# Cross attention: a longer ring of key chunks, both copies of the keys' high part in one load, and a head's output four pairs later

## The chip, the cores and the metric

The kernel runs on one core of a Trainium2 chip. The time is the device time of one execution in microseconds (us), from the first to the last instruction with what lies around it. The engines are named as in the profile: PE is TensorE (PEld its weight loads), DVE is VectorE, ACT is ScalarE, POOL is GpSimd, and SP is SyncE, which here only issues DMAs.

## The reference

The program is a perceiver of two layers on 512 latent rows of 512 numbers. Each layer has a cross attention to a context of 8192 rows, a mixer (a selective scan in layer 0, linear attention in layer 1), and a feed-forward part with experts. The change touches the two cross attentions alone. With 16 heads of 32 numbers they compute

```python
# layer 0, and layer 1 without the mask
energy = jnp.einsum('nqhd,nkhd->nhqk', q, k)
energy = jnp.where(mask == 0, jnp.float32(-1e+20), energy)
attention = jax.nn.softmax(energy / scale, axis=3)
out = jnp.einsum('nhql,nlhd->nqhd', attention, v).reshape(n, q_len, EMBED)
return out @ Wo.T + bo
```

All of it is in float32. Keys and queries are split into a high and a low part. The product is taken as one matmul over 98 rows (QROWS + 2): three groups of 32 rows hold the keys as high, high, low and the queries as high, low, high. The two last rows take away the largest score of each query.

## The kernel before

A head's 8192 keys are cut into 16 chunks of 512 (NKC), and a chunk into two pairs of 128-key tiles, so a head has 32 pairs (PAIRS, `p` from 0 to 31). For each chunk PE does four matmuls for the row maxima (`maxima`, line 588), which run 17 chunks (NKC + LEAD) ahead of its four matmuls for the scores (`scores`, line 610, in layer 0 each behind one that adds the mask, line 609). DVE reduces the maxima (line 744 in layer 1, 748 in layer 0). ACT takes the exponentials of a pair into one of `n_p` buffers called `prob` (line 698). PE multiplies them with the values once per chunk (`wave`, line 623).

The sums of the exponentials (the denominators) are taken over pairs. POOL adds most pairs itself (lines 855 and 858). The others it hands to DMAs that add into `den_dma` (lines 847 and 851): 9 of 32 pairs in layer 0, and 13 in layer 1 with two accumulators. At the start of the next head, one DMA for each accumulator adds it into `den_pool` (`merge`, line 836). A `prob` buffer is free again when its wave and its addition are done.

The keys lie in HBM as a high and a low matrix. SP loads each chunk into a slot of `k_ring` (`load_k`, line 544): three loads of 32 rows of 2 KB, two of them the same high rows. The ring has 19 slots (KRING), and chunk n + 19 is loaded when the scores of chunk n are done. PE needs it at the start of chunk n + 2. At chunk 1 of each head SP also loads the queries of the head after next (line 535) and the next head's values (line 550, 1 MB). All of SP's loads go through one queue. POOL's additions by DMA go through another, and both are served by the same 16 DMA engines.

When a head's waves are over, `head_out` (line 636, at pair 8 of the next head) turns its output and sums the denominators. It waits for the merges. ACT copies the result (`head_rows`, line 709), and DVE adds the parts at pair 11 (`den_sum`), with a division every fourth head (line 777).

Each engine's order is the order of its own function in the code. Engines wait for each other by semaphores alone.

Of the kernel before, what the change touches and what calls it, by code (L numbers as in the profile page):

```python
# [30 lines left out]
LEAD = 1  # L31
KRING = NKC + LEAD + 2
KT = S2 // P
# [444 lines left out]
def cross_attention(k, ctx, q_hi_lo, k_hi_lo, v_heads, v_first, w_out, bias, x_rows, comb, scale, masks, attT):  # L478
# [7 lines left out]
    rows_m = slice(QROWS, QROWS + 2)  # L486
    n_q, n_p = 3, 6 if masked else 8
    q_stack = [k.sbuf(ctx, "q_stack", [QROWS + 2, T], F32R) for _ in range(n_q)]
    k_ring = k.sbuf(ctx, "k_ring", [QROWS + 2, KRING, KC], F32R)
    v_buf = [v_first[:].rearrange("p k n -> p (k n)"), k.x[:].rearrange("p i d -> p (i d)")]  # L490
# [5 lines left out]
    den_dma = [k.sbuf(ctx, "den_dma", [P, 2, T], F32) for _ in range(sums.n_acc)]  # L496
    small = k.sbuf(ctx, "bias_and_m_hi", [QROWS + 2, T], F32)
    bias_row, m_hi = small[0:1, :], small[rows_m, :].bitcast(F32R)
    den4 = k.sbuf(ctx, "den_of_4_heads", [P, T], F32)
    lo_sign = k.sbuf(ctx, "lo_sign", [QROWS + 2, 1], F32)  # L500
    o_sb = k.sbuf(ctx, "o_sb", [P, T], F32)

    s_k = [k.sem("s_k") for _ in range(KRING)]
    s_v = [k.sem("s_v") for _ in range(2)]
# [22 lines left out]
    with nc.Block() as block:  # L527
        @block.sync
        def _(e):
# [8 lines left out]
            def load_k(n):  # L538
                h, c = divmod(n, NKC)
                rows = slice(h * DH, (h + 1) * DH)  # L540
                if n >= KRING:
                    e.wait_ge(s_score, 2 * (n - KRING) + 2)
                for g, part in enumerate((0, 0, 1)):
                    e.dma_start(k_ring[g * DH:(g + 1) * DH, n % KRING, :].bitcast(F32),
                                k_hi_lo[part][rows, chunk_cols(c)]).then_inc(s_k[n % KRING], 16)

# [5 lines left out]
            load_q(0)  # L552
            for n in range(KRING):
                load_k(n)
            load_q(1)
            load_v(0)
            for n in range(NCH):
                h, c = divmod(n, NKC)
                if n + KRING < NCH:
                    load_k(n + KRING)  # L560
                if c == 1 and h + 2 < H:
                    load_q(h + 2)
                if c == 1 and h == H - 1:
                    e.wait_ge(s_wave, WAVES * (H - 1))
                    e.dma_start(v_first[:], w_out).then_inc(s_wo, 16)
                    e.dma_start(bias_row, bias).then_inc(s_bo, 16)
                elif c == 1:
                    load_v(h + 1)
            e.wait_ge(s_wave, WAVES * H)
            e.dma_start(k.x[:], x_rows).then_inc(s_xback, 16)  # L570
# [3 lines left out]
        def _(e):  # L574
            def maxima(n, i):
                h, c = divmod(n, NKC)
                if i == 0:
                    if c == 0:
                        e.wait_ge(s_q[h % n_q], 48 * (h // n_q + 1))
                    if c == 0 and h >= n_q:  # L580
                        e.wait_ge(s_zero, h - n_q + 1)
                    if n < KRING:
                        e.wait_ge(s_ring, n_q + n + 1)
                    e.wait_ge(s_k[n % KRING], 48 * (n // KRING + 1))
                if 4 * n + i >= 2:
                    e.wait_ge(s_red, 4 * n + i - 1)

                e.matmul(k.bank(maxbank[i % 2]), q_stack[h % n_q][:, i * P:(i + 1) * P], k_ring[:, n % KRING, :],  # L588
                         start=True, stop=True).then_inc(s_max, 1)
# [9 lines left out]
            def scores(g):  # L599
# [6 lines left out]
                for j in range(2):  # L606
                    kt = 2 * j2 + j
                    if masked:
                        e.matmul(k.bank(kt), k.ident_big[:], masks[1][:, 2 * p + j, :], start=True, stop=False)  # L609
                    ins = e.matmul(k.bank(kt), k_ring[:, n % KRING, kt * P:(kt + 1) * P], q_stack[h % n_q][:],  # L610
                                   start=not masked, stop=True)
# [32 lines left out]
            for g in range(H * PAIRS):  # L644
# [12 lines left out]
                if p == PAIRS - 2 and h + 1 < H:  # L657
                    max_rows(h + 1)
                if p == 8 and h > 0:
                    head_out(h - 1)  # L660
# [16 lines left out]
        def _(e):  # L677
            mask_rows = k.i["mask"].rearrange("(i p) k -> p i k", p=P)

            def m_hi_rows(h):  # L680
                e.wait_ge(s_topT, h + 1)
                if h > 0:
                    e.wait_ge(s_mlo, h)
                e.activation(m_hi, misc[rows_m, :], ACT.Copy).then_inc(s_mhi, 1)

# [36 lines left out]
            for g in range(H * PAIRS):  # L722
# [4 lines left out]
                if p == 1 and h > 0:  # L727
                    take_values(h - 1)
                if p == 8 and h > 0:
                    head_rows(h - 1)  # L730
# [4 lines left out]
        def _(e):  # L735
# [23 lines left out]
            def m_lo_rows(h):  # L759
                e.wait_ge(s_mhi, h + 1)  # L760
                if h >= n_q:
                    e.wait_ge(s_score, reused_stack(h))
                e.scalar_tensor_tensor(out=q_stack[h % n_q][rows_m, :], in0=small[rows_m, :], scalar=lo_sign[rows_m, :],
                                       in1=misc[rows_m, :], op0=ALU.mult, op1=ALU.add).then_inc(s_mlo, 1)
# [29 lines left out]
            for g in range(H * PAIRS):  # L794
# [11 lines left out]
                if p == 3 and n_q <= h + 2 < H:  # L806
                    zero_rows(h + 2)
                if p == 11 and h > 0:
                    den_sum(h - 1)
# [10 lines left out]
        def _(e):  # L820
# [3 lines left out]
            for b in range(n_q):  # L824
                e.memset(q_stack[b][rows_m, :].bitcast(F32), 0.0).then_inc(s_ring, 1)
            for n in range(KRING):
                e.memset(k_ring[rows_m, n, :].bitcast(F32), -1.0).then_inc(s_ring, 1)
            e.wait_ge(s_ring, n_q + KRING)

# [1878 lines left out]
```

## Time and profile before

| | us |
|---|---|
| median of 3 runs | 4746.3 (4741.35 to 4748.71) |
| the profiled execution, its own time | 4741.35 |
| its span, first to last instruction | 4739.6 |
| layer 0, cross attention, first matmul of line 588 to last of line 610 | 406.0 to 1591 |
| layer 1, the same | 2691.9 to 3802.6 |

The profile is of the fastest of the three runs, and 1.75 us of its time lie around the span. The span's busy shares are PE 87%, PEld 47%, DVE 64%, ACT 45%, POOL 44%. The granted TensorE clock is 0.92 of full speed over the span. A row of a timeline reads: start, duration, engine, line, operation, tiles written and read, and in brackets how long the engine had been idle and for what.

### The profile page before, as it was taken

Reading aid. Unit: us, or ns where it says so; the run is one execution under the profiler, and the core shown is the slowest. Engines: PE = TensorE matmul, PEld = TensorE weight load, DVE = VectorE, ACT = ScalarE, POOL = GpSimd, SP = SyncE. Lnnn points to the kernel's source line nnn. Section 1 sums busy time; section 2 is a strip of 40 time slices with the busy share of each in tenths; the row PEclk is TensorE's granted clock in tenths of the full one; section 3 lists DMA queues with packets and bytes.
Section 4 is the critical chain, followed back from the end, with each engine's and each line's share of the span. In section 5 each row is a group of like instructions: output and inputs, shape, how many; then the busy total and the mean of one; then the engine's idle time right before and its main releaser. Section 6 shows DMA issues by size and latency. Waiting matters only on the chain. (4 is left out here: it accounts for less than half of the span.)

```text
span 4739.6 us, 50995 instructions
## 1 busy us (share of the span) xinstructions
PE 4103.6 (87%) x17384; PEld 2236.5 (47%) x17384; DVE 3035.5 (64%) x5059; ACT 2130.9 (45%) x2348; POOL 2068.5 (44%) x1208
## 2 busy tenths in 40 slices
PE   8995999999999686689999588888888879669997
PEld 6883444443434251157777343333333323347775
DVE  4335777777777259945777476666766543377776
ACT  2220444554545333324767145455555623146675
POOL 0000788888889616400000168778887920000000
PEclk9996999999999779889999789899998979889998
DMA  8997565665655300024888468778887840307876
GB/s 299 338 330 257 125 141 128 142 144 128 142 136 131 102 13 0 0 82 154 303 302 311 146 144 186 174 176 186 175 190 179 179 111 0 99 9 281 304 301 234
DMA packets 294006, 803.62 MB, mean 170 GB/s; under 512 B 47475, under 2 KB 81011, under 8 KB 256372
## 3 DMA queue, kind: packets, MB, share of 16 engines
q1 hardware_dynamic: 223764, 561.77, 34.7%
q0 software_dynamic: 61280, 221.80, 23.3%
q10 hardware_dynamic: 8704, 16.78, 1.1%
q8 instruction: 141, 2.31, 0.2%
q14 instruction: 117, 0.96, 0.1%
HBM read 485.81 MB, written 98.37 MB: 123 GB/s over the span
## 5 line engine op out<-in xcount | busy, mean ns | idle before, releaser
L588 PE MATMUL psum<-k_ring,q_stack 98*128 98x512 f32 x2048 | 916.5, 471 | 218.6 <-DMA k_ring<-k_lo 132.9
L858 POOL TENSOR_TENSOR den_pool<-den_pool,prob 128x1024 f32<-128x1024 f32 x418 | 1022.2, 2445 | 146.4 <-ACT prob L698 128.0
L698 ACT ACTIVATE prob<-psum 128x1024 f32<-128x1024 f32 x726 | 741.9, 1024 | 697.1 <-PE psum L610 658.5
L744 DVE TENSOR_REDUCE row_max<-psum 128x1 f32<-128x512 f32 x1024 | 682.5, 689 | 326.8 <-PE psum L588 322.6
L748 DVE CUSTOM_DVE_ANT_0 psum<-psum,mask_q 128x512 f32<-128x512 f32 x1024 | 703.1, 707 | 291.4 <-PE psum L588 289.7
L610 PE MATMUL psum<-q_stack,k_ring 98*128 98x512 f32 x2048 | 884.3, 504 | 2.8 <-ACT prob L698 2.5
L588 PEld LDWEIGHTS psum<-k_ring,q_stack 98*128 98x128 f32 x2048 | 409.2, 200 | 932.7 <-issue 339.0
L1814 DVE TENSOR_TENSOR weight_lo<-weight_raw,weight_hi 128x2048 fp32r<-128x2048 f32 x240 | 547.0, 2290 | 162.2 <-ACT weight_hi L1757 161.9
L858 POOL TENSOR_TENSOR den_pool<-den_pool,xnT 128x1024 f32<-128x1024 f32 x190 | 465.0, 2447 | 62.2 <-ACT xnT L698 52.3
L1757 ACT ACTIVATE weight_hi<-weight_raw 128x2048 fp32r<-128x2048 f32 x240 | 453.9, 1915 | 39.3 <-DMA weight_raw<-in_L_ffn_w 22.4
L698 ACT ACTIVATE xnT<-psum 128x1024 f32<-128x1024 f32 x298 | 304.7, 1024 | 297.6 <-PE psum L610 276.8
L610 PEld LDWEIGHTS psum<-q_stack,k_ring 98*128 98x128 f32 x2048 | 413.0, 203 | 47.2 <-ACT prob L698 17.6
L609 PE MATMUL psum<-mask_k,ident_big 128*128 128x512 fp8e4 x1024 | 405.9, 396 | 6.9 <-ACT xnT L698 5.0
L1670 POOL DMA_DIRECT2D y_slots<-xnT x30 | 16.4, 545 | 878.9 <-ACT xnT L1779 878.9
L1256 PE MATMUL psum<-dB_u,ident 128*128 128x512 f32 x256 | 156.3, 710 | 99.5 <-DVE dB_u L1231 99.3
L1217 POOL TENSOR_TENSOR dB_u<-delta_u,B_all 128x2048 f32<-128x2048 f32 x32 | 144.2, 4513 | 196.9 <-POOLq L1099 109.5
L847 POOL DMA_DIRECT2D den_dma<-prob x228 | 204.0, 895 | 52.3 <-ACT prob L698 31.2
L609 PEld LDWEIGHTS psum<-mask_k,ident_big 128*128 128x128 bf16 x1024 | 100.9, 99 | 245.4 <-issue 213.9
L104 PE MATMUL psum<-weight_hi,hidden_T_hi 128*128 128x512 f32 x480 | 199.1, 415 | 3.8 <-DVE weight_lo L1814 3.5
L104 PE MATMUL psum<-weight_hi,slot_x_hi 128*128 128x512 f32 x480 | 201.6, 420 | 0.0
L623 PE MATMUL psum<-prob,v_then_wo 128*32 128x512 f32 x1448 | 201.3, 629 | 0.0
L623 PE MATMUL psum<-prob,x 128*32 128x512 f32 x1456 | 196.9, 613 | 0.0
(398 smaller groups left out, 6354.1 us busy)
## 6 DMA issues: line engine op xcount, KB each, us to landing
den_dma<-prob POOLq DMA_DIRECT2D x254, 512.0 KB, 5.0
weight_raw<-in_L_ffn_w SPq DMA_DIRECT2D x120, 1024.0 KB, 6.5
k_ring<-k_hi SPq DMA_DIRECT2D x1024, 64.0 KB, 2.7
weight_raw<-in_L_ffn_Wu SPq DMA_DIRECT2D x60, 1024.0 KB, 7.1
weight_raw<-in_L_ffn_Wd SPq DMA_DIRECT2D x60, 1024.0 KB, 5.0
den_dma<-xnT POOLq DMA_DIRECT2D x98, 512.0 KB, 4.9
k_ring<-k_lo SPq DMA_DIRECT2D x512, 64.0 KB, 2.6
den_pool<-den_dma POOLq DMA_DIRECT2D x48, 512.0 KB, 5.6
```

The lines of the kernel that those rows point to most:

```text
L104: ins = e.matmul(out, lhsT, rhs, start=start and n == 0, stop=stop and n == len(terms) - 1)
L588: e.matmul(k.bank(maxbank[i % 2]), q_stack[h % n_q][:, i * P:(i + 1) * P], k_ring[:, n % KRING, :], start=True, stop=True).then_inc(s_max, 1)
L609: e.matmul(k.bank(kt), k.ident_big[:], masks[1][:, 2 * p + j, :], start=True, stop=False)
L610: ins = e.matmul(k.bank(kt), k_ring[:, n % KRING, kt * P:(kt + 1) * P], q_stack[h % n_q][:], start=not masked, stop=True)
L623: ins = e.matmul(vbank[n * DH:(n + 1) * DH, :], v_buf[h % 2][:, t * DH:(t + 1) * DH], prob[(PAIRS * h + t // 2) % n_p][:, t % 2, :], start ...
L698: e.activation(prob[g % n_p], k.psum[:, 2 * j2:2 * j2 + 2, :], ACT.Exp, scale=scale).then_inc(s_exp, 1)
L744: e.reduce_max(out, bank, AXIS_X).then_inc(s_red, 1)
L748: e.tensor_tensor_reduce(out=bank, in0=bank, in1=masks[0][:, i, chunk_cols(c)], scale=1.0, scalar=-3.0e38, op0=ALU.add, op1=ALU.max, accum ...
L847: e.dma_start(den_dma[a][:], tile, accum_op=ALU.add).then_inc(s_ddma[a], 16)
L858: e.tensor_tensor(den[:], den[:], tile, ALU.add).then_inc(s_dpool, 1)
L1757: e.activation(hi[q % RING][:], raw[q % RAW][:], ACT.Copy).then_inc(s_whi, 1)
L1814: e.tensor_tensor(lo[q % RING][:], raw[q % RAW][:], hi[q % RING][:].bitcast(F32), ALU.subtract).then_inc(s_wlo, 1)
```

## The change

- The ring gets 20 slots in layer 0 and 32 in layer 1. In layer 1 `n_p` goes from 8 to 10.
- The two loads of the same high rows become one, whose source names the 32 rows twice (`to_broadcast([2, DH, KC])`, a first dimension of size 2 and step 0). Its destination is the first 64 rows of the slot. The slot's semaphore then counts two loads.
- `head_out` and `head_rows` move from pair 8 to pair 12, `den_sum` and the division from pair 11 to 15.
- The tile `small` is gone. ACT writes the rounded maximum straight into the rows of `q_stack`, where DVE reads it and puts the remainder in its place. Two waits go with it. The bias row is loaded into a part of `den_pool` at the end of the last head.
- POOL sets the two last rows of each slot once at the start: 20 and 32 memsets in place of 19 each.

```diff
--- before.py
+++ after.py
-KRING = NKC + LEAD + 2
...
-    n_q, n_p = 3, 6 if masked else 8
+    n_q, n_p = 3, 6 if masked else 10
+    kring = NKC + LEAD + (3 if masked else 15)
     q_stack = [k.sbuf(ctx, "q_stack", [QROWS + 2, T], F32R) for _ in range(n_q)]
-    k_ring = k.sbuf(ctx, "k_ring", [QROWS + 2, KRING, KC], F32R)
+    k_ring = k.sbuf(ctx, "k_ring", [QROWS + 2, kring, KC], F32R)
...
-    small = k.sbuf(ctx, "bias_and_m_hi", [QROWS + 2, T], F32)
-    bias_row, m_hi = small[0:1, :], small[rows_m, :].bitcast(F32R)
+    bias_row = den_pool[0][0:1, 0, :]
...
-                if n >= KRING:
-                    e.wait_ge(s_score, 2 * (n - KRING) + 2)
-                for g, part in enumerate((0, 0, 1)):
-                    e.dma_start(k_ring[g * DH:(g + 1) * DH, n % KRING, :].bitcast(F32),
-                                k_hi_lo[part][rows, chunk_cols(c)]).then_inc(s_k[n % KRING], 16)
+                if n >= kring:
+                    e.wait_ge(s_score, 2 * (n - kring) + 2)
+                hi, lo = (part[rows, chunk_cols(c)] for part in k_hi_lo)
+                e.dma_start(k_ring[0:2 * DH, n % kring, :].bitcast(F32), hi.unsqueeze(0).to_broadcast([2, DH, KC])
+                            ).then_inc(s_k[n % kring], 16)
+                e.dma_start(k_ring[2 * DH:QROWS, n % kring, :].bitcast(F32), lo).then_inc(s_k[n % kring], 16)
...
                     e.dma_start(v_first[:], w_out).then_inc(s_wo, 16)
-                    e.dma_start(bias_row, bias).then_inc(s_bo, 16)
                 elif c == 1:
                     load_v(h + 1)
+            e.wait_ge(s_head, H - 1)
+            e.dma_start(bias_row, bias).then_inc(s_bo, 16)
...
-                    e.wait_ge(s_k[n % KRING], 48 * (n // KRING + 1))
+                    e.wait_ge(s_k[n % kring], 32 * (n // kring + 1))
...
-                if p == 8 and h > 0:
+                if p == 12 and h > 0:
                     head_out(h - 1)
...
-                if h > 0:
-                    e.wait_ge(s_mlo, h)
-                e.activation(m_hi, misc[rows_m, :], ACT.Copy).then_inc(s_mhi, 1)
+                e.activation(q_stack[h % n_q][rows_m, :], misc[rows_m, :], ACT.Copy).then_inc(s_mhi, 1)
...
-                if p == 8 and h > 0:
+                if p == 12 and h > 0:
                     head_rows(h - 1)
...
-                if h >= n_q:
-                    e.wait_ge(s_score, reused_stack(h))
-                e.scalar_tensor_tensor(out=q_stack[h % n_q][rows_m, :], in0=small[rows_m, :], scalar=lo_sign[rows_m, :],
+                m_rows = q_stack[h % n_q][rows_m, :]
+                e.scalar_tensor_tensor(out=m_rows, in0=m_rows.bitcast(F32), scalar=lo_sign[rows_m, :],
                                        in1=misc[rows_m, :], op0=ALU.mult, op1=ALU.add).then_inc(s_mlo, 1)
...
-                if p == 11 and h > 0:
+                if p == 15 and h > 0:
                     den_sum(h - 1)
...
-            for n in range(KRING):
+            for n in range(kring):
                 e.memset(k_ring[rows_m, n, :].bitcast(F32), -1.0).then_inc(s_ring, 1)
```

SP's queue at the start of layer 0's cross attention, before. A row is an operation with its destination, source and the destination's shape:

```order
L535 DMA q_stack<-q_hi 32x512
L535 DMA q_stack<-q_lo 32x512
L535 DMA q_stack<-q_hi 32x512
L544 DMA k_ring<-k_hi 32x512 x2
L544 DMA k_ring<-k_lo 32x512
L544 DMA k_ring<-k_hi 32x512 x2
L544 DMA k_ring<-k_lo 32x512
L544 DMA k_ring<-k_hi 32x512 x2
```

and now:

```order
L534 DMA q_stack<-q_hi 32x512
L534 DMA q_stack<-q_lo 32x512
L534 DMA q_stack<-q_hi 32x512
L543 DMA k_ring<-k_hi 64x1x512
L545 DMA k_ring<-k_lo 32x512
L543 DMA k_ring<-k_hi 64x1x512
L545 DMA k_ring<-k_lo 32x512
L543 DMA k_ring<-k_hi 64x1x512
```

The two loads of 32 high rows have become one to 64 rows, and line numbers are one less.

ACT in head 1 of layer 0 before, from the exponentials of pairs 2 and 3 (in `xnT`, two of the `prob` buffers) to head 0's output rows (`attT` and `den_of_heads`):

```order
L698 ACTIVATE xnT<-psum 128x1024 x2
L698 ACTIVATE prob<-psum 128x1024 x4
L698 ACTIVATE xnT<-psum 128x1024
L709 ACTIVATE attT<-psum 32x512
L712 ACTIVATE den_of_heads<-psum 32x512
L698 ACTIVATE xnT<-psum 128x1024
```

and now:

```order
L697 ACTIVATE xnT<-psum 128x1024 x2
L697 ACTIVATE prob<-psum 128x1024 x4
L697 ACTIVATE xnT<-psum 128x1024 x2
L697 ACTIVATE prob<-psum 128x1024 x3
L708 ACTIVATE attT<-psum 32x512
L711 ACTIVATE den_of_heads<-psum 32x512
L697 ACTIVATE prob<-psum 128x1024
```

Four more exponentials stand ahead of the head's output rows. PE's `head_out` moves in the same way.

## Rows read from the trace of the kernel before

**Rows 1.** The profile's page: the span and the costliest group.
```profile
span 4739.6 us, 50995 instructions
...
L588 PE MATMUL psum<-k_ring,q_stack 98*128 98x512 f32 x2048 | 916.5, 471 | 218.6 <-DMA k_ring<-k_lo 132.9
```

**Rows 2.** Busy time by stretch: 14 heads of layer 0, 14 of layer 1.
```profile
core 0: us, PE busy (x) PEld busy (x) DVE busy (x) ACT busy (x) POOL busy (x), PEclk, DMA share, GB/s
552.70:1537.00 984.30, 940.43 (x4674) 404.17 (x4673) 710.35 (x1859) 491.80 (x504) 844.81 (x448) 0.99 0.60 137
2809.80:3755.50 945.70, 831.19 (x3777) 366.21 (x3775) 651.27 (x968) 491.85 (x504) 765.98 (x462) 0.93 0.80 181
```

**Rows 3.** PE's waits, 500 to 1550 us (total, times, longest).
```profile
PE psum L588 <- DMA k_ring<-k_lo: 28.7, 26, 3.0
```

**Rows 4.** PE's waits, 2790 to 3790 us.
```profile
PE psum L588 <- DMA k_ring<-k_lo: 71.4, 50, 4.9
PE psum L636 <- DMA den_pool<-den_dma: 18.8, 13, 6.2
```

**Rows 5.** Timeline of SP, layer 1: start, duration; a chunk is released between them.
```profile
3115.57 1.51 SPq L544 DMA_DIRECT2D k_ring<-k_hi  x2
...
3118.97 1.44 SPq L544 DMA_DIRECT2D k_ring<-k_hi  x2
```

**Rows 6.** Timeline of SP, layer 0, the same.
```profile
597.75 0.77 SPq L544 DMA_DIRECT2D k_ring<-k_hi  x2
...
601.75 0.77 SPq L544 DMA_DIRECT2D k_ring<-k_hi  x2
```

**Rows 7.** Timeline, layer 1, chunks 1 to 4 of a head.
```profile
3022.15 0.53 SPq L550 DMA_DIRECT2D x<-v_heads  x1
...
3023.78 0.50 PE L588 MATMUL psum<-k_ring,q_stack 98*128 98x512 f32 x1 [0.96 <-DMA k_ring<-k_lo]
...
3029.21 0.50 PE L588 MATMUL psum<-k_ring,q_stack 98*128 98x512 f32 x1 [1.96 <-DMA k_ring<-k_lo]
...
3031.95 1.03 PE L636 MATMUL psum<-o_sb,comb 128*32 128x512 f32 x1 [1.54 <-DMA den_pool<-den_dma]
```

**Rows 8.** DMA queues (packets, MB, share of 16), layer 0, 500 to 1550 us.
```profile
q0 software_dynamic: 21600, 78.65, 38.4%
q1 hardware_dynamic: 38326, 64.96, 21.6%
```

**Rows 9.** DMA queues, layer 1 (2790 to 3790 us).
```profile
q0 software_dynamic: 32167, 117.16, 59.5%
q1 hardware_dynamic: 37106, 62.96, 20.4%
```

**Rows 10.** DMA, 2700 to 2720 us: packets by size, loads issued.
```profile
DMA packets 1881, 2.73 MB, mean 137 GB/s; under 512 B 624, under 2 KB 624, under 8 KB 1857
...
k_ring<-k_hi SPq DMA_DIRECT2D x22, 64.0 KB, 2.1
...
k_ring<-k_lo SPq DMA_DIRECT2D x12, 64.0 KB, 2.0
```

**Rows 11.** DMA, 2121.9 to 2126.5 us: packets by size.
```profile
DMA packets 321, 0.18 MB, mean 39 GB/s; under 512 B 48, under 2 KB 304, under 8 KB 320
```

**Rows 12.** DMA, 2204.4 to 2207 us: packets, and a load of two rows.
```profile
DMA packets 37, 0.27 MB, mean 106 GB/s; under 512 B 2, under 2 KB 2, under 8 KB 4
...
up_b_row<-up_bias SPq DMA_DIRECT2D x1, 4.0 KB
```

**Rows 13.** DMA queue of SP, 2300 to 2600 us (weights).
```profile
q1 hardware_dynamic: 12430, 89.17, 79.7%
```

**Rows 14.** DMA queue of SP, 100 to 300 us (context).
```profile
q1 hardware_dynamic: 46821, 65.54, 94.5%
```

**Rows 15.** Timeline of POOL, layer 1, last head: first and last additions.
```profile
3758.50 2.39 POOL L855 TENSOR_TENSOR den_pool<-prob 128x1024 f32<-128x1024 f32 x1
...
3809.77 5.56 POOL L858 TENSOR_TENSOR den_pool<-den_pool,xnT 128x1024 f32<-128x1024 f32 x2
```

## What the change should do to the time

> **What bounds the kernel now.** I read three views: busy time by stretch, then what PE waited for in each stretch, then the DMA queues. The chain that ended last covers only the final normalization and says nothing here. The page names line 588 as PE's costliest group, with 132.9 of its 218.6 us of idle time spent waiting for keys [rows 1]. The first view gives the time of a head. From the first score of head 1 to that of head 15, layer 0 takes 984.3 us and layer 1 945.7 us for 14 heads each: POOL's 448 instructions are 14 times 32 and its 462 are 14 times 33. That is 70.3 and 67.6 us a head [rows 2]. PE is busy 96% of layer 0's stretch and 88% of layer 1's, and the granted clock is 0.99 and 0.93.
>
> An undisturbed chunk shows in SP's own timeline. The load of a chunk goes out when the scores of one are done, so two of these starts lie a chunk apart: 3.40 us in layer 1 [rows 5] and 4.00 us in layer 0 [rows 6]. Sixteen make 54.4 and 64.0 us, so 13 us a head in layer 1 and 6 us in layer 0 are something else. The second view says what. PE stood idle for keys 28.7 us in 26 places of layer 0 [rows 3], and 71.4 us in 50 places of layer 1, where it also waited 18.8 us for the merges [rows 4]. The timeline shows one such place. SP issues the 1 MB of values, the keys behind them come late twice (0.96 and 1.96 us), and at pair 8 the head's output waits 1.54 us for a merge [rows 7]. So a longer ring and a later output aim at waits that are there.
>
> The third view decides the case. In layer 1 POOL's queue takes 59.5% of the 16 DMA engines and SP's queue 20.4% [rows 9]; in layer 0 it is 38.4% and 21.6% [rows 8]. The engines have room as long as each load spreads over all of them.
>
> **The double load.** How many engines a load used can be read from the packets. Between 2700 and 2720 us SP issued 38 loads (34 of keys, 3 of queries, 1 of values), and 624 packets were under 512 B, though no data of these loads is that small [rows 10]. That is 16 a load: each engine that takes part ends with one small packet. At 2122 us stand two loads of 128 rows and two of 8 rows, and the small packets are 48, which is 2 times 16 and 2 times 8 [rows 11]. A load of two rows leaves two small packets and two of data [rows 12]. So the engines follow the first dimension: 8 rows use 8 engines, 2 rows use 2. The new load has 64 rows at its destination, but its source's first dimension is 2. No load of before has two sides that differ so. I take the smaller, two engines, since the small first dimensions in these rows set the number each time.
>
> The Trainium skill, "DMA: Bandwidth & Descriptors", in "Why a DMA increments its semaphore by 16 and not by 1", says that a DMA runs on the largest number up to 16 that divides the first dimension (size 1 left out) of both sides, and its "Rules for kernel authors" name this very case: a leading broadcast of c copies confines the whole DMA to at most c engines. It would give two engines, and rows 10 to 12 agree with it where both sides are alike.
>
> The cost is the work of those two engines. Each moves half of the 128 KB of a chunk, 0.0655 MB, and 1.049 MB a head. One engine's time for 1 MB follows from a queue's share times 16 times the stretch, over its MB. With weights it is 0.797 x 16 x 300 / 89.17 = 42.9 us [rows 13], with the context 0.945 x 16 x 200 / 65.54 = 46.1 us [rows 14], and in layer 1 now 0.204 x 16 x 1000 / 62.96 = 51.8 us [rows 9]. A head's double loads then take 45.0, 48.4 or 54.4 us of each of the two engines. I take 45.0, the price under a queue that never runs dry, because this one won't.
>
> The rest of their work stays. POOL's queue takes 0.595 x 67.6 = 40.2 us a head in layer 1 and 0.384 x 70.3 = 27.0 us in layer 0. SP's queue takes 13.8 and 15.2 us, of which the high keys are 2.10 of 4.39 MB (48 loads of 64 KB, 3 of queries, 1 MB of values), so 7.2 and 7.9 us are left. The sums are 40.2 + 7.2 + 45.0 = 92.4 us a head in layer 1, and 27.0 + 7.9 + 45.0 = 79.9 us in layer 0. Both are above the 67.6 and 70.3 us of now. A ring can bridge a late load but not a rate, so the two engines set the pace: a chunk every 5.8 and 5.0 us. Keys of 240 of the 256 chunks are due in the 15 heads after the start, hence 15 x 24.8 = 372 us in layer 1 and 15 x 9.6 = 144 us in layer 0.
>
> **The other parts.** The longer ring and the two added `prob` buffers would take away the waits for keys, but not under this rate: nothing. The later output lies four pairs behind the merge's landing; its 18.8 us are also inside heads that the two engines now stretch: nothing. SP issues two loads for three; its queue is not late. Dropping `small` leaves ACT's and DVE's instructions as many and as wide as before. The 13 more memsets of layer 1 run while PE goes through the 17 first chunks, 58 us. The bias row goes out at pair 12 of the last head, over 30 us before its matmul. All of these count nothing, and if one does cost, it is under 5 us. The division every fourth head (three waits of DVE's maxima in each layer) moves with its pair and stays.
>
> The sum against the profiled execution (4741.35 us, its span 4739.6) is 4741 + 372 + 144 = 5257 us; I say 5260. The median of the runs is 5 us above that execution, which is well inside the range.
>
> **Rivals.** *All 16 engines serve the double load* (12 in 100). The destination's 64 rows would decide it. Nothing in rows 10 to 12 excludes this for two unlike sides. Then the waits go. POOL alone needs 3758.50 to 3815.3 = 56.8 us for layer 1's last head, where it hardly waits [rows 15], and PE needs 54.4 us and some 3 for the change of heads, the output and the division. With 2 us of leftovers a head takes 59.5 us, 8.1 less. Layer 0 comes to 64.0 + 4 = 68.0, 2.3 less. That is 15 x 10.4 = 156 us: 4585 us, faster.
>
> *Two engines, but not the bound* (6 in 100). If an engine served SP's packets while one of POOL's adding packets waits, its time would be the larger of the two and not the sum: 7.2 + 45.0 = 52 us a head, under 59.5. Against it stands that no queue's share plus the other's passes 100% in any row I have. The time would be some 4600 to 4650 us, faster. It decides from the point where the sum falls below 67.6 us, that is where under 20 of POOL's 40.2 us exclude SP's.
>
> *Two engines, and the clock goes too* (inside the forecast's case, its upper end). PE would wait 1 to 2 us in each chunk. Now the clock is already 0.93 in layer 1, where waits are more frequent, against 0.99 [rows 2]. In layer 1 a slower PE hides behind 5.8 us a chunk. In layer 0, 5.0 us leave 1.0 us over the 4.00, and a part of the chunks would run longer.
>
> **How the numbers follow.** The forecast's case, that two engines set the pace, has 80 in 100. Its own bounds are these. With the dearest price, 54.4, the heads take 101.8 and 89.3 us, which gives 4741 + 513 + 285 = 5540. With 45.0 and a tenth of the work overlapping on an engine, they take 83.2 and 71.9 us, or 4741 + 234 + 24 = 5000. The range is 5000 to 5550, and it leaves out the two faster rivals. The last 2 in 100 go to offsets that cancel. A measurement of this kernel tells about 0.2% from no change, 10 us. So faster has 0.18, same 0.01, slower 0.81.
>
> **What would show it.** If I am right, small packets of SP's queue fall to 2 + 16 a chunk instead of 48. The double load lands after 5 us and more where one took 2.1 [rows 10]. Line 588 waits for `k_ring` in nearly every chunk, longer in layer 1. Starts of SP's key loads lie 5 to 6 us apart, POOL waits for ACT, and the DMA share falls although two engines are full. If line 588 hardly waits, and heads take about 60 us in layer 1, the first rival is right and my step on the source's first dimension is wrong. If small packets show 2 engines and heads still take 60 to 67 us, it is the second: adding packets and loads overlap.

## The result and the profile after

The changed kernel takes 5128.1 us (median of 4 runs, 5120.59 to 5139.64), the kernel before beside it 4747.51 us (4741.35 to 4751.46). The ratio is 1.0805, with a 95% interval of 1.0779 to 1.0831. The profiled execution took 5120.59 us, 379 more than that of before. The forecast was 5260 us with a range of 5000 to 5550.

The page of the changed kernel: span, packets, and PE's costliest group ([rows 1] before). Line 588 of before is 589 here, 610 is 611, 636 is 637, 698 is 697, and SP's key loads stand in lines 543 and 545.

```profile
span 5118.5 us, 50455 instructions
...
DMA packets 278641, 803.50 MB, mean 157 GB/s; under 512 B 32115, under 2 KB 65652, under 8 KB 241013
...
L589 PE MATMUL psum<-k_ring,q_stack 98*128 98x512 f32 x2048 | 947.2, 489 | 403.2 <-DMA k_ring<-k_lo 227.1
```

Packets under 512 B were 47475 before and are 32115 now. The difference is 15360, which is 512 chunks times 30, so a chunk leaves 18 small packets for 48. That is 16 for the low keys and 2 for the double load: two engines carry it, as the third view of the kernel before had suggested. PE's idle time ahead of the maxima rose from 218.6 to 403.2 us.

Busy time by stretch, from the first score of head 1 to that of head 15 in each layer ([rows 2] before):

```profile
core 0: us, PE busy (x) PEld busy (x) DVE busy (x) ACT busy (x) POOL busy (x), PEclk, DMA share, GB/s
582.70:1665.60 1082.90, 982.49 (x4674) 415.96 (x4673) 709.99 (x1859) 485.09 (x504) 848.66 (x447) 0.95 0.52 125
2980.00:4129.70 1149.70, 897.11 (x3776) 400.41 (x3774) 647.68 (x968) 490.66 (x504) 782.30 (x467) 0.83 0.62 149
```

A head takes 1082.9 / 14 = 77.4 us in layer 0 (70.3 before) and 1149.7 / 14 = 82.1 us in layer 1 (67.6 before). The DMA share fell, from 0.60 and 0.80 to 0.52 and 0.62, although the kernel waits more. An average over 16 engines hides two that are full. The trace's own packets, taken from start to end, show this. In the changed kernel's stretch of layer 1 fewer than two packets are under way at once in under 0.1% of the time, and exactly two in 32%. In the kernel before it was 14% and 1%. The granted clock is 0.95 and 0.83, for 0.99 and 0.93.

DMA of layer 1, heads 1 to 13: packets, MB and share of 16 engines; then KB and median us to landing ([rows 9] before).

```profile
q0 software_dynamic: 28469, 103.64, 46.6%
q1 hardware_dynamic: 26898, 56.14, 15.5%
...
den_dma<-prob POOLq DMA_DIRECT2D x136, 512.0 KB, 7.8
...
v_then_wo<-v_heads SPq DMA_DIRECT2D x7, 1024.0 KB, 16.4
```

These 1079.4 us hold 13 heads of 83.0 us. POOL's queue takes 0.466 x 83.0 = 38.7 us of each engine, SP's 0.155 x 16 x 83.0 = 206 us of all together. Taking away the 7.2 us an engine that I had put down for SP's other loads (115 us on 16) leaves 91 us for the double load, or 45.4 us on each of its two engines. The forecast had used 45.0. The sum is 38.7 + 7.2 + 45.4 = 91.3 us, and the head takes 83.0: about a tenth of the work overlaps. This is an estimate, because no view separates the double loads from SP's other loads.

What PE and SP waited for in that layer (total, times, longest; [rows 4] before):

```profile
PE psum L589 <- DMA k_ring<-k_lo: 122.1, 54, 4.4
PE psum L589 <- DMA q_stack<-q_hi: 80.5, 12, 10.2
PE psum L637 <- DMA den_pool<-den_dma: 20.6, 14, 9.2
```

```profile
SPq L543 <- PE psum L611: 33.5, 57, 2.2
```

SP waits for a free chunk of the ring in only 33.5 of 1150 us. Something else holds it, and its timeline (start, duration) shows what:

```profile
3686.59 7.53 SPq L545 DMA_DIRECT2D k_ring<-k_lo  x1
3694.16 0.51 SPq L543 DMA_DIRECT2D k_ring<-k_hi  x1
3694.71 4.46 SPq L545 DMA_DIRECT2D k_ring<-k_lo  x1
3699.51 0.51 SPq L543 DMA_DIRECT2D k_ring<-k_hi  x1
...
3705.91 5.92 SPq L545 DMA_DIRECT2D k_ring<-k_lo  x1
...
3712.43 6.39 SPq L545 DMA_DIRECT2D k_ring<-k_lo  x1
```

An issue of low keys that takes 0.43 us when the queue is short takes up to 7.53 us here; over the whole run the median is 1.86 us and the longest 8.98 us, where the longest issue of a key load was 2.24 us in the kernel before. SP is held while it issues. I read this as the double loads ahead of it not having gone yet. Everything that SP issues later stands behind them. That is why PE also waited 80.5 us in 12 places for the queries of a coming head (`q_stack`), a wait that the kernel before did not have in layer 1, and why the 1 MB of values lands after 16.4 us.

In layer 0 the picture is another one. There SP does wait for the ring, and ACT waits for the sums:

```profile
SPq L543 <- PE psum L611: 782.5, 218, 9.5
```

```profile
ACT prob L697 <- DMA den_dma<-prob: 155.2, 44, 5.9
...
ACT xnT L697 <- DMA den_dma<-xnT: 60.1, 19, 5.7
```

ACT cannot reuse a buffer of `prob` before POOL's adding transfer has read it. Such a transfer lands after 6.9 us in layer 0 where it took 4.8 before (median). I read this as its slices on the two engines standing behind the double loads. ACT waits 215 us for them; in the kernel before, over the same 14 heads, all waits of ACT for these transfers came to 20 us. The two engines are nearly as full in this layer: fewer than two packets are under way in 1.8% of its stretch, and in 30% before.

### The profile page after: what moved, and what is told of

The parts are those of the page before. It is cut to its first block and busy times, and to the rows that moved or that the text cites. A ratio compares the mean times of both kernels' runs of the same rounds, so it can differ in the third digit from the quotient of the medians.

```text
span 5118.5 us, 50455 instructions
## 1 busy us (share of the span) xinstructions
PE 4224.2 (83%) x17384; PEld 2286.7 (45%) x17384; DVE 3033.0 (59%) x5059; ACT 2122.9 (41%) x2348; POOL 2091.6 (41%) x1222
## 2 busy tenths in 40 slices
DMA packets 278641, 803.50 MB, mean 157 GB/s; under 512 B 32115, under 2 KB 65652, under 8 KB 241013
## 5 line engine op out<-in xcount | busy, mean ns | idle before, releaser
L589 PE MATMUL psum<-k_ring,q_stack 98*128 98x512 f32 x2048 | 947.2, 489 | 403.2 <-DMA k_ring<-k_lo 227.1
L856 POOL TENSOR_TENSOR den_pool<-den_pool,prob 128x1024 f32<-128x1024 f32 x444 | 1133.8, 2554 | 173.6 <-ACT prob L697 154.1
L697 ACT ACTIVATE prob<-psum 128x1024 f32<-128x1024 f32 x752 | 765.0, 1024 | 1014.2 <-PE psum L611 817.8
L611 PE MATMUL psum<-q_stack,k_ring 98*128 98x512 f32 x2048 | 929.0, 527 | 4.8 <-ACT prob L697 3.7
L589 PEld LDWEIGHTS psum<-k_ring,q_stack 98*128 98x128 f32 x2048 | 426.3, 209 | 1132.9 <-issue 433.9
L611 PEld LDWEIGHTS psum<-q_stack,k_ring 98*128 98x128 f32 x2048 | 435.9, 214 | 53.9 <-ACT prob L697 19.5
L856 POOL TENSOR_TENSOR den_pool<-den_pool,xnT 128x1024 f32<-128x1024 f32 x164 | 416.0, 2537 | 43.1 <-ACT xnT L697 34.1
L697 ACT ACTIVATE xnT<-psum 128x1024 f32<-128x1024 f32 x272 | 277.2, 1024 | 329.4 <-PE psum L611 237.6
L1668 POOL DMA_DIRECT2D y_slots<-xnT x30 | 16.4, 545 | 878.1 <-ACT xnT L1777 878.1
L624 PE MATMUL psum<-prob,x 128*32 128x512 f32 x1512 | 220.4, 658 | 1.4 <-ACT prob L697 1.4
L624 PE MATMUL psum<-prob,v_then_wo 128*32 128x512 f32 x1496 | 219.8, 662 | 0.0
```

Source lines behind the costliest of these rows:

```text
L611: ins = e.matmul(k.bank(kt), k_ring[:, n % kring, kt * P:(kt + 1) * P], q_stack[h % n_q][:], start=not masked, stop=True)
L624: ins = e.matmul(vbank[n * DH:(n + 1) * DH, :], v_buf[h % 2][:, t * DH:(t + 1) * DH], prob[(PAIRS * h + t // 2) % n_p][:, t % 2, :], start ...
L697: e.activation(prob[g % n_p], k.psum[:, 2 * j2:2 * j2 + 2, :], ACT.Exp, scale=scale).then_inc(s_exp, 1)
L856: e.tensor_tensor(den[:], den[:], tile, ALU.add).then_inc(s_dpool, 1)
```

## Experiments

The theory to test (A): the double load's first dimension of 2 puts it on two DMA engines, and these set the pace. The rivals: the ring or the later output costs the time (B); the row that is read twice, or a load of 64 rows, is slow in itself (C). Medians are of 4 runs or more, each compared with the kernel before on the same chip (4741 to 4750 us). "A head" is again the stretch from the first score of head 1 to that of head 15, divided by 14, layer 0 then layer 1.

| kernel | us | ratio (95%) | a head |
|---|---|---|---|
| changed kernel | 5128 | 1.0805 (1.0779-1.0831) | 77.4, 82.1 |
| three loads | 4616 | 0.9730 (0.9708-0.9751) | 67.9, 60.6 |
| double load alone | 5485 | 1.1572 (1.1531-1.1613) | 90.5, 94.4 |
| copies side by side | 4611 | 0.9719 (0.9700-0.9738) | 67.8, 59.8 |
| first dimension 2 | 5163 | 1.0885 (1.0859-1.0912) | 77.2, 84.7 |
| first dimension 4 | 4744 | 0.9989 (0.9975-1.0003) | 69.3, 67.6 |
| first dimension 8 | 4637 | 0.9781 (0.9758-0.9804) | 67.9, 60.6 |
| ring alone, three loads | 4675 | 0.9842 (0.9818-0.9866) | 67.9, 65.0 |
| later output alone, three loads | 4719 | 0.9939 (0.9917-0.9961) | 71.0, 65.2 |
| changed, ring 19 in both | 5498 | 1.1580 (1.1552-1.1609) | 92.4, 92.7 |
| changed, rings 22 and 23 | 5139 | 1.0824 (1.0797-1.0851) | 78.2, 83.4 |
| changed, early output | 5131 | 1.0814 (1.0785-1.0842) | 78.0, 81.8 |
| changed, values early | 5127 | 1.0806 (1.0780-1.0831) | 78.5, 83.0 |

### Three loads again

```diff
-    e.dma_start(k_ring[0:2 * DH, n % kring, :]..., hi.unsqueeze(0).to_broadcast([2, DH, KC]))
+    for g in range(2):
+        e.dma_start(k_ring[g * DH:(g + 1) * DH, n % kring, :]..., hi)
```

> The changed kernel with its double load split again into two loads of 32 rows; the rings of 20 and 32 chunks, the two more buffers of prob and the output at pair 12 stay. Theory A (two DMA engines carry the double load and set the pace): all of the loss goes with this one edit. The small packets are 48 a chunk again (about 47500 in all), a head takes 70 us or less in layer 0 and 60 to 67 us in layer 1, and the time is 4600 to 4760 us. Rival B (the longer ring, whose 32 chunks go out ahead of the queries and the values, or the later output costs the time): it stays at 5050 us or more.

4615.81 us, 512 us under the changed kernel. Its page, and its windows:

```profile
DMA packets 294006, 803.61 MB, mean 174 GB/s; under 512 B 47475, under 2 KB 81012, under 8 KB 256373
```

```profile
core 0: us, PE busy (x) PEld busy (x) DVE busy (x) ACT busy (x) POOL busy (x), PEclk, DMA share, GB/s
554.40:1504.50 950.10, 934.98 (x4674) 402.55 (x4673) 711.70 (x1859) 491.79 (x504) 846.84 (x448) 0.99 0.62 142
2779.40:3627.60 848.20, 789.65 (x3777) 352.94 (x3775) 661.16 (x968) 491.81 (x504) 770.26 (x461) 0.97 0.87 199
```

The small packets are the 47475 of before, the DMA share in layer 1 is 0.87, and the ring with the later output is worth 128 us over the kernel before. B is out: all of the loss goes with this one line.

### The double load alone

The kernel before with the changed kernel's two loads for its three (ring 19, 8 buffers of `prob` in layer 1, output at pair 8).

```diff
-    for g, part in enumerate((0, 0, 1)):
-        e.dma_start(k_ring[g * DH:(g + 1) * DH, n % KRING, :]..., k_hi_lo[part][rows, chunk_cols(c)])
+    e.dma_start(k_ring[0:2 * DH, n % KRING, :]..., hi.unsqueeze(0).to_broadcast([2, DH, KC]))
+    e.dma_start(k_ring[2 * DH:QROWS, n % KRING, :]..., lo)
```

> The kernel before with the double load alone: ring of 19 chunks, 8 buffers of prob in layer 1, output at pair 8. Theory A: the small packets are 18 a chunk, a head takes about 77 us in layer 0 and 83 us in layer 1, as in the changed kernel, and the time is 5080 to 5200 us: the start of layer 1, where the changed kernel loses 31 us behind its 32 chunks, should cost less, and the shorter ring should cost some of it back. Rival B (ring or output): 4740 to 4780 us.

5485.18 us, above the range that I gave. The double load costs 741 us by itself, and the other parts of the change give 357 us of that back. The forecast had counted them as nothing under the double load. The experiment on the ring, below, takes this up.

### The copies side by side

```diff
-    hi.unsqueeze(0).to_broadcast([2, DH, KC])      # source dimensions 2, 32, 512
+    hi.unsqueeze(1).to_broadcast([DH, 2, KC])      # source dimensions 32, 2, 512
```

The queries' high and low rows go to even and odd rows of `q_stack` to match.

> The changed kernel, with the two copies of a row written beside each other: the one load still reads each high row twice and moves the same bytes, but its source's first dimension is 32 and the copies are the second one. The queries' high and low rows are laid out in the same order. Theory A: 16 engines take part, the small packets are 32 a chunk (about 39300 in all), and the time is that of three loads or a little less, 4600 to 4760 us. Rival C (reading one row twice, or one load of 64 rows, is what is slow): it stays at 5050 us or more.

```profile
DMA packets 285808, 803.53 MB, mean 174 GB/s; under 512 B 39283, under 2 KB 72819, under 8 KB 248180
```

4610.54 us. It is still one load that reads each row twice and writes 64 rows, and the bytes are the same. The small packets are 39283, which is 7168 = 512 x 14 more than in the changed kernel: 32 a chunk for 18, so 16 for this load. C is out as well. This is the fastest kernel of the study, 2.8% under the kernel before, though level with three loads within the intervals: a load fewer a chunk is worth nothing that can be told here.

### First dimension 2, 4 and 8, no row read twice

Two plain loads of the high keys, whose source is only taken in another order of rows (a = 2, 4, 8; `q_stack` laid out alike):

```diff
+    for g in range(2):
+        e.dma_start(k_ring[g * DH:(g + 1) * DH, n % kring, :]..., hi.rearrange("(b a) n -> a b n", a=2))
```

> The changed kernel with two plain loads of the high keys and no row read twice by one load, but each load's rows are taken in an order that makes its source's first dimension 2 (even rows, then odd rows; the queries' first two groups are laid out alike). Theory A, with both loads on the same two engines: 20 small packets a chunk (about 33100 in all) and a time like the changed kernel's, 5050 to 5200 us. If loads of two engines fall on different engines each time, the packets are the same and the time is 4600 to 4800 us. Rival C (a row read twice is what is slow): 4600 to 4760 us with 48 small packets a chunk.

5162.91 us: as slow as the changed kernel and 35 us more, without any repeated row. The added time lies in layer 1 (84.7 us a head for 82.1), and no view tells what of it is the extra load and what the queries. The small packets:

```profile
DMA packets 278772, 803.53 MB, mean 156 GB/s; under 512 B 32243, under 2 KB 65779, under 8 KB 241140
```

They are 32243, 128 more than the changed kernel's: the extra load adds 2 a chunk (+1024), and the 64 loads of queries that were taken in the same order leave 2 each for 16 (-896). I had left the queries out of the expectation's 33100. That separate loads do not fall on separate pairs is concluded from the time: 84.7 us a head in layer 1, where four engines for each load give 67.6 in the next run.

> As the two plain loads whose first dimension was 2, with 4. Theory A: four engines carry each load, the small packets are 24 a chunk (about 33500 in all, with the queries' 64 loads at 4 for 16), and the work on each of the four is half: 40.2 + 7.2 + 22.5 = 69.9 us a head in layer 1 if nothing overlaps, about 61 with the overlap that the pair showed (83.2 for 92.4), so that they hardly bound. The time is 4630 to 4760 us. Rival (the order of the rows, and not the number of engines, is slow): 5000 us or more.

4744.28 us. The packets, and what PE waited for in layer 1:

```profile
DMA packets 280949, 803.56 MB, mean 169 GB/s; under 512 B 34419, under 2 KB 67955, under 8 KB 243316
```

```profile
PE psum L641 <- DMA den_pool<-den_dma: 84.9, 11, 9.9
```

34419 small packets are 2304 above the changed kernel's: 6 a chunk (3072) less 12 for each of 64 loads of queries (768). So four engines carry each load. The packets under way say so too: exactly four in 16% of layer 1's stretch, and in 2% of the changed kernel's. Four do not bound the keys any more, but they still make the sums late: PE waits 84.9 us for merges, against 17.7 us with three loads. A head takes 67.6 us where I had estimated about 61. The time is inside the range, at its upper end.

> As the two plain loads whose first dimension was 2 and 4, with 8. Eight engines carry each load; with four it was 4744 us and with 16 it was 4616 us. Theory A: what an engine has to do is halved again, and the time is 4625 to 4680 us; the small packets are 32 a chunk, about 38800 in all. Rival (any order of rows but the plain one costs the same 128 us): 4730 to 4750 us.

4636.61 us, with 38771 small packets. Compared through the kernel before, eight engines cost 0.5% over sixteen (0.9781 to 0.9730). The loss falls with the number of engines: with 2, 4 and 8 it is 547, 128 and 21 us over three plain loads by the medians, and 548, 123 and 24 us compared through the kernel before.

### Ring alone and later output alone, with three loads

The first is the changed kernel with three loads and the output back at pair 8. It keeps the rings of 20 and 32 chunks, the 10 buffers of `prob` in layer 1, and `small` stays gone. The second is the kernel before with only these lines changed:

```diff
-                if p == 8 and h > 0:
+                if p == 12 and h > 0:
                     head_out(h - 1)
...
-                if p == 11 and h > 0:
+                if p == 15 and h > 0:
                     den_sum(h - 1)
```

> The kernel before (three loads of 32 rows, output at pair 8) with the rings of 20 and 32 chunks and 10 buffers of prob in layer 1. With three loads the changed kernel ran in 4616 us, 129 us under the kernel before. If the ring brings it: the waits for keys (28.7 and 71.4 us) go, and the time is 4630 to 4670 us. If the later output brings it: 4710 to 4745 us.

> The kernel before with the head's output, its rows and its sum four pairs later, and nothing else. If the ring brings the 129 us: the 18.8 us for merges in layer 1 go and some of it turns into longer waits for keys, 4725 to 4745 us. If the later output brings it: 4650 to 4690 us.

4674.92 and 4718.52 us: 75 and 32 us under the kernel before, and together 128. The ranges did not hold for either. PE's waits in layer 1, with the ring alone, with the later output alone, and with both:

```profile
PE psum L638 <- DMA den_pool<-den_dma: 72.6, 14, 6.9
```

```profile
PE psum L588 <- DMA k_ring<-k_lo: 68.7, 47, 5.4
```

```profile
PE psum L638 <- DMA den_pool<-den_dma: 17.7, 8, 3.1
```

With the ring alone, the keys are no longer in the list and the merges have grown to 72.6 us, from 12.6 us over the same 14 heads in the kernel before. With the output alone the merges are gone and 68.7 us of keys stay. The two waits hid each other, so the pair is worth more than its parts.

### Ring of 19 under the double load

```diff
-    kring = NKC + LEAD + (3 if masked else 15)
+    kring = NKC + LEAD + 2
```

> The changed kernel, double load kept, with a ring of 19 chunks in both layers; 10 buffers of prob and the output at pair 12 stay. The double load alone on the kernel before cost 741 us, the whole change 384 us, so the other parts were worth 357 us under it. Theory D (a chunk's load goes out only when one is used up, and with three chunks of lead the two engines run dry while SP waits; a longer ring keeps them full): a head takes some 95 us in layer 1, and the time is 5300 to 5480 us; in layer 0, where the ring is only one chunk shorter than the changed kernel's, a head takes between 77 and 90 us. Rival (the two engines' rate alone sets the pace, and it was the later output that helped): 5120 to 5170 us.

5498.47 us, as slow as the double load alone. So it is the ring, not the output or `prob`, that gave back the 357 us. PE's and SP's waits in layer 1, and a piece of SP's timeline:

```profile
PE psum L589 <- DMA k_ring<-k_lo: 339.0, 151, 7.6
```

```profile
SPq L543 <- PE psum L611: 975.6, 211, 11.1
```

```profile
3705.87 0.62 SPq L545 DMA_DIRECT2D k_ring<-k_lo  x1
3713.00 0.51 SPq L543 DMA_DIRECT2D k_ring<-k_hi  x1
3713.55 0.43 SPq L545 DMA_DIRECT2D k_ring<-k_lo  x1
3719.70 0.51 SPq L543 DMA_DIRECT2D k_ring<-k_hi  x1
```

SP waits for a chunk of the ring 975.6 of 1297 us, where it waited 33.5 with 32 chunks, and its issues of low keys take 0.46 us (median of the run; 1.86 in the changed kernel): the queue is short. Yet PE waits 339.0 us for keys in 151 places. With two chunks of lead a load goes out late, takes its time on the slow pair, and the pair then stands idle until PE has used the next chunk. In layer 0, one chunk of ring (19 for 20) is worth 15 us a head. The idle pair is shown for a part of this. Fewer than two packets are under way in 5.0% of layer 1's stretch (4.6 of the 10.6 us that a head is longer than in the changed kernel) and in 10.8% of layer 0's (8.6 of the 15 us). This is the least that the pair can have been idle, since other engines' packets can hide more. The rest stays open.

### Rings of 22 and 23 under the double load

```diff
-    n_q, n_p = 3, 6 if masked else 10
-    kring = NKC + LEAD + (3 if masked else 15)
+    n_q, n_p = 3, 5 if masked else 10
+    kring = NKC + LEAD + (5 if masked else 6)
```

> The changed kernel, double load kept, with rings of 22 chunks in layer 0 (20 in the changed kernel; for the room, 5 buffers of prob for 6 there) and 23 in layer 1 (32). Theory D (with few chunks of lead the two engines run dry between loads): layer 0, where SP still waited for PE 588 of 800 us, gains, 70 to 76 us a head for 77, unless the lost buffer of prob eats it; layer 1 lies between the 93 us of 19 chunks and the 83 us of 32. If the rate is what is left from 7 chunks of lead on, it is 83 to 86 us there, and the time is 5050 to 5180 us. Rival (layer 0 is bound by late sums and not by its ring): its heads take 77 us or more, and the time is 5150 to 5250 us.

5139.43 us. Layer 1 takes 83.4 us a head: from 23 chunks on, the rate of the two engines is all that is left, and nine more chunks give a microsecond. Layer 0 takes 78.2 us, which is the rival's number, though the time of the run is not in the rival's range. Its waits:

```profile
PE psum L610 <- ACT prob L697: 60.6, 33, 3.9
PE psum L610 <- ACT xnT L697: 40.7, 22, 3.4
```

```profile
ACT prob L697 <- DMA den_dma<-prob: 195.4, 52, 7.4
...
ACT xnT L697 <- DMA den_dma<-xnT: 131.1, 34, 6.7
```

The longer ring took the last 28 us of waits for keys away, and waits for ACT, who waits for the sums, came in their place. The missing buffer of `prob` makes that heavier (326 us of ACT's waits for 215), so that this run does not tell what 22 chunks with 6 buffers would give.

### Early output under the double load

The changed kernel with `head_out`, `head_rows` and `den_sum` at pairs 8, 8 and 11 again (the reverse of the diff above).

> The changed kernel, double load kept, with the head's output back at pair 8 (and its rows and sum with it). With three loads the later output was worth 59 us (4675 to 4616 us). If the two engines' rate hides all else, as the prediction counted: 5120 to 5140 us. If it is worth as much under the double load as under three: 5180 to 5190 us. A merge waits for a sum that lands after 7.7 us and not 5.0, so that it could be worth more: above 5200 us.

```profile
PE psum L637 <- DMA den_pool<-den_dma: 110.7, 14, 16.3
...
PE psum L589 <- DMA k_ring<-k_lo: 56.7, 30, 4.6
```

5130.72 us, no difference. PE waits 110.7 us for merges where it waited 20.6, and 56.7 us for keys where it waited 122.1. When a transfer rate sets the pace, a wait that is added elsewhere on PE is taken from the wait for keys. With three loads the same edit was worth 59 us.

### Values and queries ahead of the later chunks

```diff
             load_q(0)
             for n in range(kring):
+                if n == NKC:
+                    load_q(1)
+                    load_v(0)
                 load_k(n)
-            load_q(1)
-            load_v(0)
```

> The changed kernel, double load kept, with the queries of head 1 and the values of head 0 issued after the first 16 chunks of keys, not after all 20 or 32. In the changed kernel layer 1 takes 90.3 us from its first maximum to the scores of head 1 (58.8 before), and PE stands 32.1 us once for the queries of head 1. Theory E (that wait is the queries behind 32 double loads in SP's queue): the 31 us go, layer 0's start hardly changes, and the time is 5085 to 5105 us. Rival (the start is short of keys themselves): the wait moves to the keys and the time stays at 5115 to 5140 us.

The start of layer 1 in the changed kernel, first maximum to the first score of head 0, was 90.3 us for 58.8 before, which the forecast had not seen. (The expectation calls this span one to the scores of head 1; its two numbers end at head 0.) PE's waits there, in the changed kernel and in this one:

```profile
PE psum L589 <- DMA q_stack<-q_hi: 32.1, 1, 32.1
PE psum L589 <- DMA k_ring<-k_lo: 16.8, 1, 16.8
```

```profile
PE psum L590 <- DMA k_ring<-k_lo: 16.8, 1, 16.8
```

The 32.1 us for the queries are gone, and the start takes 58.8 us. But the time is 5127.42 us, the same. Heads 0 and 1 then take 67.4 and 88.7 us, where they took 56.8 and 68.3. In the changed kernel, as I read it, the two engines had filled the ring while PE stood, and the heads lived on that store. Layer 1 gained 9 us of the 31 up to head 15, and layer 0 took 14 more, which is not explained. The place of the wait moved and its size hardly did. I had priced a wait as though it were on the path, and it was the two engines' work seen from PE.

## Why the prediction was right, and where it was not

**Two engines, from small packets and first dimensions.** Right: 18 a chunk in the changed kernel, and the same slow kernel from any first dimension of 2, with or without a row that is read twice. The smaller of two unlike sides decides, which no load of the kernel before could show (in every run the smaller side also divides the larger, so nothing here tells it from a common divisor); the copies side by side, with 32 on the source and 64 at the destination, run on all 16. The rule of the Trainium skill, "DMA: Bandwidth & Descriptors", "Why a DMA increments its semaphore by 16 and not by 1", agrees with all four counts (2, 4, 8 and 16).

**The price of the work.** 45.0 us a head on each of the two engines was used; 45.4 is what the shares of layer 1 give, and the start of layer 1 gives 16 x 2.64 = 42 us (last section). The term was right for this kernel. It is not a fixed price. With the ring of 19 the same working gives 59.5 us for the double loads and 38.1 + 7.2 + 59.5 = 104.8 us of work in a head of 92.7, and packets of 2 KB take 113 ns in the mean there and 94 ns in the changed kernel. What was too high is the plain sum of an engine's work: 92.4 us a head was forecast, 82.1 measured, and 83.2 was the low bound, "45.0 and a tenth of the work overlapping". For layer 1 that bound should have been the value. From its first maximum to the scores of head 15, it took 1296.8 us for 1063.6, 233 more, where 372 were forecast. The rest of the 379 us is 122 in layer 0 and 24 outside these two stretches. That 5128 us lies so near to 5260 is in part luck: the starts of the two layers, which the forecast took as unchanged, took 31 and 18 us more and made up for a part of the overlap that it had left out.

**Layer 0.** 79.9 us a head forecast, 77.4 measured, and over the same stretch of the layer 122 us for 144. The size is near, the picture was only half right. I had PE short of keys in every chunk. It waited 28 us for keys in 14 heads, as before. The crowded pair shows as late sums: ACT waits for buffers, and PE for ACT (57 us, 4 of the 7 us that a head grew). Besides, PE is busy 982 us for 940 in these 14 heads at the clock of 0.95, the other 3 us. The forecast had named the clock for its upper end only.

**The other parts count nothing.** This step failed for the ring. "The longer ring and the two added `prob` buffers would take away the waits for keys, but not under this rate: nothing", but without the ring the same double load costs 741 us and not 381. A rate bounds only an engine that always has work; with 19 chunks the pair runs dry while SP waits, shown above for about half of the loss. The sum was computed for full engines, which they are because of the longer ring. For the later output the step held: 5131 to 5128 us.

**Signs to look for.** Small packets and the falling DMA share came as named. The 5 to 6 us between SP's key loads hold only in the mean: in the piece of the timeline above, two starts lie 5.4 us apart, at the start of the layer 2.3 to 2.9 us, and the mean is 82.1 / 16 = 5.1 us. When a double load lands cannot be read: the profile gives no landing for it. "Line 588 waits for `k_ring` in nearly every chunk" was wrong: 54 places in layer 1 (224 chunks). PE stands once for 10.19 us until 3719.49 us, for the queries, and then goes on to 3765 us without a wait for keys, which the ring of 32 had taken in meanwhile:

```profile
3719.49 0.79 PE L589 MATMUL psum<-k_ring,q_stack 98*128 98x512 f32 x1 [10.19 <-DMA q_stack<-q_hi]
...
3765.95 0.50 PE L589 MATMUL psum<-k_ring,q_stack 98*128 98x512 f32 x1 [0.79 <-DMA k_ring<-k_lo]
```

That it would stand for queries, behind keys that it did not need yet, I had not seen. POOL's waits for ACT came: 180 us in layer 1's stretch for 95 in its adding line before. In the reading of [rows 10], the 38 loads leave 608 small packets; the other 16 of the 624 fit one key load issued just ahead of the window.

**The first rival** was sized well: all 16 engines, 59.5 and 68.0 us a head and 4585 us. The kernel with the copies side by side has 16 engines and takes 59.8 and 67.8 us a head and 4611 us. The second rival (heads of 60 to 67 us on two engines) is out with 82.1 us.

## What to carry to other kernels

Before two loads are joined into one, look at the outermost dimension of both sides: put the long one there, and keep a repeat inside it. A small outermost dimension costs twice, once in its own bytes and once in every other transfer that has a slice on the same engines, and a mean DMA share falls while it happens. Find out whether a late transfer is short of rate or of lead. If the issuer waits for room while its consumer waits for its loads, it is lead, and a longer ring helps (layer 1 with 19 chunks). If the issuer is held in its issue, it is rate (layer 1 with 32). Waiting for room alone says nothing: in layer 0 SP waited 782.5 us for the ring, PE only 28 us for keys, and two more chunks with a buffer of `prob` less gained nothing. When a rate sets the pace, waits on the waiting engine are only names for it, and removing one moves it.

## What the hardware showed that I had not expected

- An issue of low keys on SP takes 0.43 us when its queue is short and up to 8.98 us behind double loads. At the start of layer 1, with every chunk of the ring free, it starts one chunk in 2.3 to 2.9 us:

```profile
2835.52 0.51 SPq L543 DMA_DIRECT2D k_ring<-k_hi  x1
...
2837.80 0.51 SPq L543 DMA_DIRECT2D k_ring<-k_hi  x1
...
2840.67 0.50 SPq L543 DMA_DIRECT2D k_ring<-k_hi  x1
...
2843.25 0.50 SPq L543 DMA_DIRECT2D k_ring<-k_hi  x1
...
2848.72 0.51 SPq L543 DMA_DIRECT2D k_ring<-k_hi  x1
```

Over five chunks that is 13.2 us, or 2.64 us for the 0.0655 MB of each of the two engines: 40 us a MB, a little under the 42.9 of [rows 13].

- A POOL transfer of 512 KB over 16 engines lands 7.8 us after its issue in layer 1 (5.6 us with three loads), though 14 of its 16 engines have less to do.
- Four engines for the high keys lose again all that the longer ring and the later output give (4744 us, the kernel before), and eight are nearly as good as sixteen (4637 to 4616 us).
- With three loads, the waits for keys and for merges each hid behind the other: 75 us and 32 us alone, 128 us together.
